# First places of two experts by matrix products, whole-row head norm on ScalarE, and moved weight transposes in a four-block transformer kernel

## What is computed

```python
x = x + _L0_xattn_ref(_layernorm(x), ctx, ctx, ...)   # gated linear attention, 4 heads of 64, head norm
x = x + _L0_ffn_ref(_layernorm(x), ...)               # quantised gated feed-forward, 768 hidden
x = x + _L1_xattn_ref(_layernorm(x), ctx, ctx, ...)   # softmax attention, 16 heads of 16
x = x + _L1_ffn_ref(_layernorm(x), w_router, wi, wo)  # router, 8 experts
```

```python
router_probs = softmax(x @ w_router)                  # 8 logits for each token
gate, idx = top_k(router_probs, 2)
pos = cumsum(mask_kt, axis=1) * mask_kt - 1.0         # place of a token in its expert, per group of 1024
dispatch, combine = one-hot of pos (160 places for each of 2 groups)
h = relu(expert_in @ wi)                              # 256 -> 1024
y = combine @ (h @ wo)                                # 1024 -> 256, weighted by the gate
```

## Time and profile before

| | us |
|---|---|
| median of 3 executions | 591.28 (590.52 to 592.04) |
| profiled execution, its own time | 594.54 |
| its span on the core | 592.8 |
| TensorE (PE) busy | 519.8 (88%) |
| VectorE (DVE) busy | 381.6 (64%) |
| ScalarE (ACT) busy | 327.0 (55%) |
| GpSimd (POOL) busy | 142.5 (24%) |

### The profile page before, as it was taken

The page is one execution under the profiler, slowest core; times in us unless marked ns, Lnnn a source line. Parts: engine busy times, 40 slices in busy tenths (PEclk is TensorE's granted clock), DMA queues, the critical chain, the costliest instruction groups (busy, mean ns, idle before and its releaser), DMA issues.

```text
span 592.8 us, 9394 instructions
## 1 busy us (share of the span) xinstructions
PE 519.8 (88%) x3362; PEld 372.6 (63%) x3362; DVE 381.6 (64%) x980; ACT 327.0 (55%) x697; POOL 142.5 (24%) x202
## 2 busy tenths in 40 slices
PE   1989996899999700999999999998999999999994
PEld 1568864654444300887757678777788777677773
DVE  6576889845389989788688699987732232233101
ACT  2857577723389969680389799997122212211220
POOL 2006544000000000000332232211245344534441
PEclk9989999999999955699999999999799999999998
DMA  7910000000000000016000011014215645353410
GB/s 221 305 19 1 2 1 0 2 0 1 0 0 1 1 0 0 1 46 239 2 0 2 1 39 36 2 37 159 52 46 170 200 132 195 121 181 124 132 46 22
DMA packets 32013, 37.62 MB, mean 63 GB/s; under 512 B 8672, under 2 KB 27744, under 8 KB 31968
## 3 DMA queue, kind: packets, MB, share of 16 engines
q1 hardware_dynamic: 28896, 29.07, 15.3%
q0 software_dynamic: 3072, 7.95, 4.3%
HBM read 30.14 MB, written 6.88 MB: 62 GB/s over the span
## 4 chain that ended last, share of the span: by engine, by line
PE 71%; DVE 14%; ACT 9%; issue 2%; POOL 2%; POOLq 0%; DVEq 0%
PE pA L2203 12%; PE pB L2233 10%; PE pC L1869 6%; PE pC L1908 5%; PE pA L1902 3%; PE pB L1918 3%; PE pC L2217 3%; PE pA L1824 2%; PE pB L1824 2%; PE pC L1824 2%; ACT XIT L748 2%; DVE am L1259 2%; DVE arena L1255 2%; PE pB L1998 2%; DVE am L1225 2%
## 5 line engine op out<-in xcount | busy, mean ns | idle before, releaser
L499 POOL TENSOR_TENSOR arena<-KT,par 128x256 f32<-128x256 f32 x32 | 19.0, 615 | 248.6 <-DVE XIT L1333 186.7
L2203 PE MATMUL pA<-arena 128*128 128x320 f32 (+2 forms) x320 | 75.7, 387 | 0.5 <-ACT arena L923 0.5
L937 ACT ACTIVATE arena<-pA 128x320 f32<-128x320 f32 (+2 forms) x80 | 30.7, 384 | 73.0 <-PE pA L2203 67.5
L2203 PEld LDWEIGHTS pA<-arena 128*128 128x128 f32 x320 | 53.7, 190 | 16.2 <-issue 1.1
L2233 PE MATMUL pB<-arena 128*128 128x256 f32 x256 | 59.8, 385 | 0.0
L2233 PEld LDWEIGHTS pB<-arena 128*128 128x128 f32 x256 | 47.2, 190 | 8.5 <-issue 2.3
L1225 DVE TENSOR_REDUCE am<-arena 128x1 f32<-128x512 f32 x48 | 32.1, 682 | 23.0 <-ACT arena L688 22.9
L1869 PE MATMUL pC<-wdnT,XIT 128*128 128x256 f32 x192 | 43.5, 384 | 0.8 <-DVE XIT L1333 0.8
L1409 DVE TENSOR_REDUCE rm<-pA 128x16 f32<-128x2048 f32 x16 | 36.7, 2291 | 8.8 <-PE pA L1902 8.8
L1869 PEld LDWEIGHTS pC<-wdnT,XIT 128*128 128x128 f32 x192 | 36.5, 193 | 6.9 <-DVE XIT L1333 1.6
L1908 PE MATMUL pC<-ident,arena 128*128 128x128 f32 x240 | 35.4, 280 | 1.5 <-ACT XIT L784 0.8
(11 more groups left out here) (338 smaller groups left out, 1147.2 us busy)
## 6 DMA issues: line engine op xcount, KB each, us to landing
arena<-in_L_ffn_wi SPq DMA_DIRECT2D x8, 1024.0 KB, 5.2
arena<-in_L_ffn_wo SPq DMA_DIRECT2D x8, 1024.0 KB
X<-in_x SPq DMA_DIRECT2D x4, 512.0 KB, 5.7
arena<-in_ctx SPq DMA_DIRECT2D x4, 512.0 KB, 7.3
out<-X SPq DMA_DIRECT2D x4, 512.0 KB, 2.9
token_rows<-arena SPq DMA_DIRECT2D x4, 512.0 KB, 4.7
arena<-in_L_ffn_w_up SPq DMA_DIRECT2D x1, 768.0 KB, 7.5
arena<-in_L_ffn_w_gate SPq DMA_DIRECT2D x1, 768.0 KB, 9.2
```

The lines of the kernel that those rows point to most:

```text
L937: nc.scalar.activation(HT[:, e % 2, f, n], ps[2 + f % 2][:, 0:n.stop - n.start], ACT.Relu).then_inc(s["h_relu"], 1)
L2203: last = mm(ps[2 + f % 2][:, 0:n.stop - n.start], WI[:, u, k, f * P:(f + 1) * P], XET[:, u, k, n], start=(k == 0), stop=(k == KD - 1))
```

## The change

Second norm. `ALL_HEADS = 13`: ScalarE norms all four heads of rows 0 to 12 (before: 0 to 7), and VectorE's `last_head` does rows 13 to 15 alone. `head_scale(0)` stands ahead of the last two roundings of weights on VectorE. `values_kept(1)` and `(2)` stand after rows 4 and 9 (before: 6 and 14). ScalarE does `keys(2)` and `keys(3)` after all head norms, then the weight copies 4 and 5 around `rsqrt(4)`; TensorE transposes those two blocks before `turn3`. The other seven stand at rows 1, 3, 5 to 13. ScalarE norms rows 4, 7, 10 and 13 (`xl_act`), with a bias that one more VectorE instruction makes.

Router. `d_logits`, `d_logits4`, their copies and transposes back are gone; all 16 rows go through `d_row`. VectorE's `last_rows_scale` (the second half of the last four rows' norm) moves from ahead of the logits to behind `less_largest(0)`.

Experts. The inputs of passes (0, A) and (1, A) come from `e_select`: for each half of the features, eight products of the rows 0 to 7 in `XR` with an f32 selection (`select_full`, in `SELF`), summed in PSUM. The token numbers are still made (from the upper halves of the same f32 words, `SELH`) and rows still gathered, for the gates and the scatter, but `e_tokens(0)`, `e_places(0)`, `e_tokens(1)`, `count(1)` and `e_places(1)` now stand inside `e_hidden(0)` and `e_out(0)`. `rows_in(1)` stands behind `sums_in(0)` on GpSimd's queue.

```diff
-        TURN_BESIDE = (0, 2, 4, 5, 7, 8, 10, 11, 13)
+        TURN_BESIDE = (-1, -1, 1, 3, 5, 7, 9, 11, 13)
+        NORM_ACT = (4, 7, 10, 13)
+        ALL_HEADS = 13
...
-                if b == 13:
-                    keys(2)
+            keys(2)
+            keys(3)
+            weights_copy(4)
             rsqrt(4, NB)
-            keys(3)
+            weights_copy(5)
+            def xl_act(b):
+                if b == NORM_ACT[0]:
+                    act.wait_ge(s["xl_scale"], 1)
+                nc.scalar.activation(at(XL, b), at(X, b), ACT.Identity, scale=rstd[:, cols(b, 1)], bias=s2[:, cols(b, 1)]).then_inc(s["xl_act"], 1)
...
-                if t in (6, 14):
-                    values_kept(1 + t // 14)
+                if t == 4:
+                    values_kept(1)
+                if t == 9:
+                    values_kept(2)
...
+            def logits(g):
+                dve.wait_ge(s["d_row"], TG * (g + 1))
+                link(V_.tensor_copy(LW[:, rows(g), :], ps[(6, 4)[g]][:, 0:TG * NE].rearrange("p (b e) -> p b e", b=TG)))
...
+            def select_full(e):
+                for b in range(TG):
+                    V_.tensor_scalar(SELF[e][:, b, :], cidx_f[:, 0, :], place[:, 0, e, b:b + 1], None, ALU.is_equal).then_inc(s["sel_full"], 1)
...
+            def d_row(b):
+                if b == 0:
+                    pe.wait_ge(s["ao_ready"], NB)
+                if b == TG:
+                    pe.wait_ge(s["x3_ready"], NB - 2)
+                pe.wait_ge(s["d_xt"], b // 2 + 1)
...
+            def e_select(i):
+                if i >= 1:
+                    pe.wait_ge(s["xet_ready"], i)
+                    pe.wait_ge(s["sel_full"], TG * (i + 1))
+                    for k in range(KD):
+                        for b in range(TG):
+                            last = mm(ps[1][:, k * P:(k + 1) * P], XR[:, b, k * P:(k + 1) * P], SELF[i][:, b, 0:P], start=(b == 0), stop=(b == TG - 1))
+                else:
+                    pe.wait_ge(s["d_xt"], 7)
+                    for b in range(TG):
+                        pe.wait_ge(s["sel_full"], b + 1)
+                        for k in range(KD):
+                            last = mm(ps[k][:, 0:P], XR[:, b, k * P:(k + 1) * P], SELF[i][:, b, 0:P], start=(b == 0), stop=(b == TG - 1))
+                last.then_inc(s["xe_tr"], 1)
...
+                            if i == 0 and f == 3:
+                                count(1)
+                                e_places(1)
+                            if i == 0 and f == 4:
+                                e_select(1)
```

More of the change, by code:

```diff
@@ L649, in head_norm @@
                 act.wait_ge(s["head_stat"], 1 + b // HB)
-                for n in range(NH0 if b < HB else NH0 - 1):
+                for n in range(NH0 if b < ALL_HEADS else NH0 - 1):
                     last = nc.scalar.activation(at(HU, b)[:, n, 0:DH0], at(HU, b)[:, n, 0:DH0], ACT.Identity, scale=rstd[:, cols(b * NH0 + n, 1)], bias=s2[:, cols(b * NH0 + n, 1)])
@@ L935, in relu @@
                 for f in range(NFT):
+                    if i == 0 and f == 5:
+                        exp4(1)
                     act.wait_ge(s["h_done"], i * NFT + f + 1)
@@ L1200, in xl_max @@
             def xl_max(b, u, h):
-                dve.wait_ge(s["xl_ready"], b + 1)
+                if b in NORM_ACT:
+                    dve.wait_ge(s["xl_act"], NORM_ACT.index(b) + 1)
+                else:
+                    dve.wait_ge(s["xl_ready"], b + 1 - sum(r < b for r in NORM_ACT))
                 V_.tensor_reduce(am[:, 0, cols(b, 1)], at(XL, b), AX.X, ALU.max, apply_absolute_value=True).then_inc(s["xl_max"], 1)
             for t in range(NB + 1):
-                if t < NB:
+                if t < NB and t not in NORM_ACT:
                     xl(t, 0, 0)
+                if t == 1:
+                    V_.scalar_tensor_tensor(out=s2[:, 0:NB], in0=mean[:, 0:NB], scalar=-1.0, in1=rstd[:, 0:NB], op0=ALU.mult, op1=ALU.mult).then_inc(s["xl_scale"], 1)
                 if t >= 1:
@@ L1582, in _ @@
             find_places(0)
[L1583 to L1584 removed]
+            select_full(0)
+            select_full(1)
+            logits(1)
             digits_kept(0)
@@ L1786, in turn3 @@
             def turn3(b):
-                pe.wait_ge(s["xl_ready"], b + 1)
+                if b in NORM_ACT:
+                    pe.wait_ge(s["xl_act"], NORM_ACT.index(b) + 1)
+                else:
+                    pe.wait_ge(s["xl_ready"], b + 1 - sum(r < b for r in NORM_ACT))
                 if b >= 2:
@@ L2119, in _ @@
             d_turn(3)
-            d_logits()
+            for b in range(TG):
+                d_row(b)
             d_turn(4)
-            d_back()
+            keep_busy(ps[7], 2)
             d_turn(5)
-            keep_busy(ps[7], 2)
-            d_logits4()
+            for b in range(TG, 12):
+                d_row(b)
             keep_busy(ps[7], 3)
-            d_back4()
-            keep_busy(ps[7], 4)
             NC = TOPK * TG * NE
@@ L2173, in e_turn @@
                         n = P if c < 2 else SHORT
-                        if part == "A":
-                            last = tr(ps[u][:, k * P:(k + 1) * P], XE[:, u, 0, k * P:(k + 1) * P], ident[:, :])
-                        else:
-                            o = c * P - places(part).start
-                            last = tr(ps[k][:, o:o + n], XE[0:n, u, c, k * P:(k + 1) * P], ident[0:n, 0:n])
+                        o = c * P - places(part).start
+                        last = tr(ps[k][:, o:o + n], XE[0:n, u, c, k * P:(k + 1) * P], ident[0:n, 0:n])
                 last.then_inc(s["xe_tr"], 1)
@@ L2186, in e_hidden @@
                 for f in range(NFT):
+                    if i == 0 and f == 1:
+                        e_tokens(0)
                     if i == 0 and f == 4:
-                        e_tokens(2)
+                        e_places(0)
+                    if i == 0 and f == 6:
+                        e_tokens(1)
                     if i == 2 and f == 4:
@@ L2211, in e_out @@
                     pe.wait_ge(s["y_ready"], PIECES[i])
+                else:
+                    pe.wait_ge(s["lg_sub"], 2)
                 if part != "A":
@@ L2236, in _ @@
             d_turn(6)
-            keep_busy(ps[7], 2)
+            keep_busy(ps[7], 3)
             d_turn(7)
+            d_row(12)
+            d_row(13)
+            keep_busy(ps[7], 4)
             count(0)
-            for b in range(12, NB):
-                d_row(b)
-            e_tokens(0)
-            e_places(0)
-            keep_busy(ps[4], 6)
-            e_tokens(1)
-            keep_busy(ps[4], 2)
-            e_places(1)
-            keep_busy(ps[4], 6)
-            count(1)
-            e_turn(0)
+            e_select(0)
+            d_row(14)
+            d_row(15)
             for i in range(len(PASSES)):
```

115 lines of the change are left out of this document (41 added, 74 removed).

## The result

The changed kernel took 596.27 us (median of 8 runs, 593.1 to 597.9) against 592.25 (8 runs, 590.5 to 593.6) for the kernel before on the same chip: ratio 1.006, interval 1.0033 to 1.0086. A repeat (experiment 5) gave 1.0056. The forecast was 595.8, which is 4.5 above the 591.28 that it started from; the measured difference is 4.0. One profiled execution, that of the repeat, was disturbed (607.99 us), and its trace is not compared with the others.

The account below looks back on a forecast made before the run. TensorE was taken as the bound, with almost no waits behind the first expert's start. Norm -1.7, router -2.5 and behind the start +4.3 gave +0.1; with the clock's +4.5, 591.28 became 595.9, stated as 595.8 us (8-in-10 range 589.0 to 600.3).

Parts of the forecast that it names:

- Norm: Second norm: TensorE's maximum comes at 115.8 against 117.57, -1.7 us, with bounds of -2.8 and -0.5.
- so the last head norm ends near 99.75 instead of 100.4: Second norm, ScalarE: starting 2.2 earlier, one more norm in rows 8 to 12, `keys(2)` moved out, about 0.9 of waiting.
- Router: Router up to the first expert's product: it starts at 422.5 instead of 425.08, -2.5 us.
- TensorE is late: Router, ahead of `count(0)`: TensorE's rows, transposes and fillers last until 416.5, 2.9 us later than VectorE.
- Behind the start: From the first expert's product on: `e_select(1)` and small products add work on TensorE, +4.3 us.
- Nothing hides it: Behind the first expert's start: the added +4.3 us shows in full, since TensorE has no waits there.
- The clock: Router: clock falls near 408 in the run of `d_row`, low 6 to 10 us, taken as 9, +4.5 us.
- Rows of 0.475 or longer: Router: a sign that each `d_row` takes 0.475 us or longer, between not slowed and doubled at the lower clock.
- The signs named ahead: Wrong if clock stays 1.00 through rows, first expert starts before 420, or start to end isn't about 4.3 us longer.
- Rival 1: Whole kernel: the clock stays up, 591.4 us, from 590 to 593; chance 0.28.
- Rival 2: Router: TensorE keeps up with VectorE ahead of `count(0)`, -5.4 instead of -2.5, total 588.5 us; chance 0.10.
- Rival 3: Clock low from 408 to the first selection's end, the second touched too: +8, 599.4 us; chance 0.14.

Follow-up runs that it names:

- experiment 5: The changed kernel measured once more without further edits, against the kernel before: 596.61 us, ratio 1.0056.
- norm_only: The kernel before with the second norm's edits alone, none of the router's: 592.83 us, ratio 0.9976 to the kernel before.
- rows128: The changed kernel with each logits-row product given 128 moving columns instead of 8: 593.73 us, ratio 0.9992 to the kernel before.
- after_full: rows128 plus ten filler products ahead of the second norm's turns: 593.68 us, ratio 1.0021 to the kernel before.
- short2: rows128 with the second expert's selection made from one tile instead of eight, output incomplete: 592.10 us, ratio 0.9975 to rows128.
- gather1: The changed kernel with `e_select(1)` removed and the second expert's rows gathered by GpSimd as before: 597.91 us, ratio 1.0066 to the kernel before.
- before_full: The kernel before with ten fillers ahead of its last values product and 128 columns in rows 12 to 15: 593.26 us, ratio 1.0006.
- early_count: rows128 with ten router fillers left out and rows 12 and 13 moved behind `e_select(0)`: 594.66 us, ratio 1.0041 to the kernel before.
- thin: The kernel before with only the router's fillers cut from 128 to 8 moving columns: 597.51 us, ratio 1.0048 to the kernel before.
- norm_fill: norm_only plus ten fillers ahead of the turns and 128 columns in rows 12 to 15: 591.65 us, ratio 0.9950 to the kernel before.
- best: early_count with the second expert gathered, its count earlier, and pass 2's digits ahead of the last selection: 592.69 us, ratio 0.9995 to the kernel before.
- hybrid: norm_fill's norm, the wide logits of the kernel before, first expert by selection products, second gathered: 590.91 us, ratio 0.9945 to the kernel before.

## Why the prediction was right, step by step

The direction and the size held, and so did the mechanism in the main: TensorE's work grows about as much as the chains shorten, and the clock falls in the run of rows. But three terms were mis-sized, and that the total came within 0.6 us is in part luck: with both kernels at full clock the sum of work and waits was taken 1.5 too low, and the clock's term, of which 2.4 is then left, 2.1 too dear.

**Norm, forecast -1.7, measured -1.07** at full clock (44.44 to 43.37). The step that failed is "so the last head norm ends near 99.75 instead of 100.4". ScalarE did start its head norms 1.84 earlier (an idle time of 2.52 instead of 4.36), but it then waited 1.50 for the next variance, where I took 0.9 and the kernel before had 0.19. With five norms more (1.7) and one `keys` less (1.15) the last head norm ends 27.15 behind ScalarE's idle point, exactly as before (88.83 and 9.72, less 71.40; 98.34 and 2.10, less 73.29). The two rows of the kernel before, ScalarE's last head norms and GpSimd's last scale:

```profile
98.34 2.10 ACT L651 ACTIVATE arena<-arena,s,rstd 128x64 f32<-128x64 f32 x6
...
100.53 0.69 POOL L487 TENSOR_TENSOR arena<-arena,oscale 128x256 f32<-128x256 f32 x1 [0.31 <-ACT arena L651]
```

The gain is the tail, where the value copies left VectorE's run: from the last scale on GpSimd to the variance's root 2.84 instead of 3.68, and 0.2 more behind it. ScalarE's row and weight copies came out as forecast, 10.9 us with the waits (forecast 10.4 and 0.4): first normed row to maximum 12.08, before 12.27.

**Router, forecast -2.5, measured -1.8** at full clock (18.96 to 17.16), -1.9 in the profiled pair with a fall in each. The forecast of the new chain was good: 17.86 from the pair transpose to the first expert's product, measured 17.16. The fault was in the other number: I compared it with the 20.44 of before, in which 1.5 was the fall at 416.5, and called the result a sum at full clock. The router of the kernel before does not fall in every execution: in norm_only, which leaves it as it was, it took 19.05 with the clock up. The claim that TensorE is late held: in rows128 the scan ends at 410.71 and the count comes at 413.09, 2.4 later (forecast 2.9), and 3.75 in the kernel after, where the fall adds the rest.

**Behind the start, forecast +4.3, measured +4.4 to +4.5**, and +5.4 in after_full. The two rows of 32 products took 3.81 and 3.73, as the earlier trace rows gave. "Nothing hides it" was right of the kernel before and right of the sum, but not of the part: short2 shows that only 1.7 of 3.1 us comes back when the products go, for VectorE's chain to the second selection is late next.

So the sum with both kernels at full clock is -1.07 - 1.8 + 4.43 = **+1.6**, not +0.1. Taken as the prediction took it, against a kernel before that has its fall in the router (17.16 - 20.44 = -3.28), it is -1.07 - 3.28 + 4.43 = **+0.1**.

**The clock, forecast +4.5 with 9 us low.** The place was right: it fell at 404.3, within the run of eight rows and with TensorE busy for 1.00 of every us. In the profiled execution it was low for 3.4 us and cost 1.37 (18.53 against 17.16). gather1's profile, with two falls, is 3.0 longer there. In the medians wide rows took back 3.8 to 4.0 us (rows128), or 2.1 to 2.3 (after_full). So the term is **+2 to +4**: this is the step that was mis-sized most, with 3.4 us low in the one profile where 9 had been taken.

What the falls of the kernel before cost decides which sum it joins. If they cost its executions the 1.5 of that profile, 0.1 and 4.0 make 4.1; if they cost nothing, 1.6 and 2.3 make 3.9. The measured difference is 4.0, and the two ways rows128 and after_full stand to the kernel before (-0.5 and +1.2 us by their ratios) fit one each. before_full can't decide it, since its clock fell elsewhere.

Seven other executions of the kernel after were 0.7 to 4.8 us longer than the profiled one; their mean clock was 0.952 to 0.963. Where their falls lay is not known. They need not be in the router: a fall near 35, one behind the maximum and the longer stretch at the lower clock in the feed-forward made the unedited parts 2, 1.6 and 1.1 us longer in other profiles, and executions of the kernel before with the same mean clock of 0.962 took from 591.6 to 594.9. So the profile accounts for 1.4 of the clock's term and the medians for all of it; where the rest lies stays open.

"Rows of 0.475 or longer" held too: the run at the lower clock took 3.85 for 32 records, hardly more than the 3.74 at full clock, since the clock fell only near its end.

**The signs named ahead.** The prediction called itself wrong if the first expert started before 420, and it started at 419.18. The bound was badly put: it took the unedited parts as fixed, and these were 1.89 and 1.06 shorter in this execution, without which it is 422.1. The forecast's 422.5 left out the norm's gain and the fall; without these, 1.04 and 1.37, the measured one is 421.8. So with the maximum: 114.89, or 116.8 less that luck (forecast 116). The other two signs spoke for it: the clock was not at 1.00 through the run of rows, and the time from that start to the end is 172.2 against 167.7, 4.5 longer (forecast 4.3).

**The rivals.** Rival 1 (the clock stays up, 591.4) was the kernel rows128, and there it came out near: 593.73 against 594.16. Rival 2 failed as forecast on the rows' time. What it asks for, an early count, was made in early_count, and the clock took it back. Rival 3 (low all the way) is what gather1's profile shows in part: 5.44 for the first selection.

The Trainium skill (TensorE: Matmul & The Clock Gate, "Why this matters for your kernels") says to keep TensorE continuously busy. Taken by the busy share that rule fails here: rows of 8 columns were busy for 1.00 and the clock fell, in the kernel after and in thin. Taken as advice to fill idle time it holds in two runs, norm_fill and after_full, where the fillers ahead of the turns kept the clock up, and not in before_full, where the clock fell at 118 instead of 102.5. In thin an idle time of 3.43 us was followed by no fall.

## What to carry to other kernels

Look at the moving columns of what keeps TensorE busy, and not at its busy share alone. Here runs of products with 8 columns were followed by the lower clock; the same runs with 128 columns took no longer (3.74 against 3.85 for 32 records) and were not (rows128, after_full). Where such a run stands on the chain that ends last, try it wide. Wide products alone are no warrant: in early_count and best, with wide rows but fewer fillers, the clock fell behind an idle time of 1.3 us.

Cut the span at points that all variants have and compare the parts; here two unedited parts varied by as much as the edit was worth. Then look at the clock in the unedited parts too: in before_full the fall had only changed its place, and the time alone looked as if falls cost nothing.

Before you fill a wait or shorten a product, ask which chain ends last at that place. Three edits made TensorE faster and got back less than they won, since its next wait grew: nothing in the norm of before_full, 1.7 of 3.1 in short2, 0.4 of 3.6 in hybrid.

## What had not been expected of the hardware

- TensorE was busy for 1.00 of every us in runs of thin products, and the clock fell all the same: the kernel before with fillers of 8 columns was low for 17.1 us behind 400 instead of 6.8, and 0.5% slower.
- A fall is not tied to a place. The same wait of 3.43 us was followed by a fall in the kernel before and by none in thin; with the wait filled (before_full) the clock fell at 118 instead of 102.5, where it cost 1.6 us instead of 0.1.
- 128x128 f32 products took 0.12 us with 8 as with 128 moving columns (3.85 / 32 and 3.74 / 32).
